# Expert phase: turning round the second layer's operands, its weights staged by ScalarE, and the first layer's weights staged by a transfer inside the chip

## The chip, the cores and the metric

One NeuronCore of a Trainium2 chip runs the whole program; the other cores stand idle. The metric is the device time of one execution in microseconds (us). Below, PE is TensorE (matrix multiplies and transposes), ACT is ScalarE, DVE is VectorE, POOL is GpSimd, SP is SyncE, which here only issues transfers and waits.

## The reference

A block of a transformer over x of 32 x 256 tokens with 128 channels (8,192 tokens): normalisation, causal attention with 16 heads, normalisation, residual; then a mixture of 8 experts, of which each token uses one; normalisation, residual. The part that matters here is the expert step.

```python
feats = x.reshape(-1, 128)
expert = argmax(feats @ centroids.T, axis=1)          # E = 8
alpha = sigmoid(sum(feats * centroids[expert], -1))
h = normalise(feats) * gamma[e] + beta[e]
y = feats + relu(h @ W1[e].T + b1[e]) @ W2[e].T + b2[e]   # W1[e]: 512 x 128, W2[e]: 128 x 512
out = alpha * y + (1 - alpha) * feats
```

## The kernel before, in words

**Attention phase.** Blocks of 256 tokens; each has 8 slots (two heads each), and every engine runs the same software pipeline over the slots. The last 16 slots (`not live(0)` in the code) only drain it, and work that prepares the expert phase is laid into them: the first layer's weights are split into two fp32r parts that add up to fp32 (`w1`, at L788 on ACT and L1005 on DVE), the biases are folded (L595 on PE), and the second bias b2 is turned into rows: eight fp32 products with the identity on PE (L711), a copy on ACT into `b2row`, and on DVE the low half and the selector `picks` (L1012, L1014). In the same slots the last two blocks are routed: each token's expert, its destination row, and a row of 260 numbers written to `routed_rows` in HBM, sorted by expert. When the count of each expert is known (`ends`, L999 on DVE), SP writes eight pads behind the experts' rows (L244), and POOL writes the last block's rows (L1210) after those have landed.

**Expert phase.** `table` gives for each of 39 tiles of 256 rows its start row and its expert. A tile goes through slots; `live(n)` in `slot` means that the tile n slots back is handled here. `ffn_phases` writes 8 slots out for the first 8 tiles, then loops over 3 x 8 slots, then writes out the rest. Order per slot s on each engine:

- SP loads the rows of tile s into `fin` (8 buffers, in the trace as `softmax`; L262), once POOL has finished with tile s-8.
- PE: two transposes of tile s into `psN` (L278), then the first layer of tile s-1: 12 fp32r matmuls, stationary `w1st`, moving the turned tokens in two parts, 256 columns each (L292), then the second layer of tile s-2: per half of 128 tokens one product with `picks` and `b2row` for the bias (L303) and four fp32 products, **stationary the hidden activations, moving the weights** straight out of `wx` at the expert's address, 128 columns (L306). The result has tokens on the partitions.
- ACT: the high part of the turned tokens (`xt_hi` in the trace), the square root for tile s-4 (`gsd`, L330), the copy of the expert's first-layer weights, 128 x 1024, into `w1st` (in the trace `p_both<-w`, two buffers), two of the four relu blocks of tile s-1 (L345), a copy of b1.
- DVE: the low part (`xt_lo`, L395), residual and statistics of tile s-3 (L405 to L415), the other two relu blocks of tile s-1 (L423), the final normalisation of tile s-4 (L429, L434).
- POOL: adds the residual for tile s-4 (L449), copies the row numbers, and scatters the tile before it to `out` with two indirect transfers (L456).

An instruction waits for semaphores by count, so the order written here is the order in which each engine runs. PE waits before L292 for the relus of tile s-2 (`relu_a`, `relu_d`), ACT before `xt_hi` for the transposes (`n_tr`).

## Time and profile before

| | us |
|---|---|
| median of 3 runs | 1291.23 (1290.55 to 1293.27) |
| the profiled execution, its own time | 1290.58 |
| its span in the trace | 1286.4 |
| PE busy | 1221.9 (95%) |
| DVE busy | 1130.4 (88%) |
| ACT busy | 1062.5 (83%) |
| POOL busy | 924.2 (72%) |

The span runs from the first to the last instruction; 4.2 us of the device time lie around it. The expert phase is what comes after 1104.7 us: the first matmul on a loaded tile starts there.

### The profile page before, as it was taken

How to read it: one execution, taken by the hardware profiler on the slowest of the kernel's cores; microseconds unless marked ns; L12 is line 12 of the kernel's file. 1: busy time of each engine (PE TensorE's matmuls, PEld its weight loads, DVE VectorE, ACT ScalarE, POOL GpSimd, SP SyncE). 2: the span in 40 equal slices, each digit the busy share in tenths (PEclk: the TensorE clock that was granted, in tenths of full speed). 3: DMA queues.
4: the chain of work that ended last, by engine and by line, in shares of the span. 5: the costliest groups of instructions: out<-in, count | busy, mean ns of one | idle time of the engine just before them, and what ended most of it. 6: DMA issues, size and time to landing. Idle time of an engine off the chain costs nothing.

```text
span 1286.4 us, 42145 instructions
## 1 busy us (share of the span) xinstructions
PE 1221.9 (95%) x12784; PEld 1105.4 (86%) x12785; DVE 1130.4 (88%) x4457; ACT 1062.5 (83%) x3244; POOL 924.2 (72%) x1495
## 2 busy tenths in 40 slices
PE   7999999999999999999999999999999997599992
PEld 6888888888888888888888888888888886599982
DVE  5999999999999999999999999999999995488873
ACT  4999898999999999999999999999999893466661
POOL 4577777777777777777777777777777665067775
PEclk8999999999999999999999999999999997799997
DMA  5000000000000000000000000000000003333320
GB/s 228 6 10 18 16 16 16 16 16 16 16 16 16 16 16 16 16 16 16 16 16 16 16 16 16 13 16 14 15 16 13 15 15 123 98 97 101 96 84 13
DMA packets 39233, 43.03 MB, mean 33 GB/s; under 512 B 4802, under 2 KB 35398, under 8 KB 38800
## 3 DMA queue, kind: packets, MB, share of 16 engines
q1 hardware_dynamic: 33536, 29.43, 7.6%
q0 software_dynamic: 5648, 13.00, 2.7%
q8 instruction: 25, 0.41, 0.1%
q14 instruction: 24, 0.20, 0.1%
HBM read 25.16 MB, written 18.16 MB: 34 GB/s over the span
## 4 chain that ended last, share of the span: by engine, by line
PE 86%; issue 5%; POOL 3%; DVE 1%; ACT 1%; SPq 1%; DMA 1%; POOLq 0%; ACTq 0%; DVEq 0%
PE psZU L682 17%; PE psS L605 14%; PE psZU L697 14%; PE psP L649 10%; PE psZU L685 7%; PE psT L619 5%; PE psT L620 5%; PE psT L621 5%; PE psS L292 3%; POOL out L456 2%; PE psZU L306 2%; PE psT L306 1%; PE psP L584 1%; PE psM L736 1%; PE psM L727 1%
## 5 line engine op out<-in xcount | busy, mean ns | idle before, releaser
L1219 POOL TENSOR_TENSOR softmax<-softmax,rinv 128x256 f32<-128x256 f32 (+1 forms) x512 | 413.2, 828 | 213.8 <-DVE rinv L947 213.0
L781 ACT ACTIVATE softmax<-softmax,nmax 128x128 f32<-128x128 f32 (+1 forms) x1024 | 453.8, 451 | 9.1 <-DVE nmax L923 8.3
L923 DVE CUSTOM_DVE_ANT_0 softmax<-psS,mask 128x128 f32<-128x128 f32 (+1 forms) x1024 | 321.6, 352 | 5.6 <-PE psS L605 1.1
L932 DVE TENSOR_TENSOR p_both<-psP,p_both 128x768 fp32r<-128x768 f32 x256 | 243.8, 952 | 0.9 <-ACT p_both L745 0.9
L745 ACT ACTIVATE t_hi<-psT 128x512 fp32r<-128x512 f32 x256 | 153.0, 598 | 84.0 <-PE psT L621 78.0
L911 DVE TENSOR_TENSOR t_lo<-psT,t_hi 128x512 fp32r<-128x512 f32 x256 | 175.3, 685 | 41.9 <-ACT t_hi L745 40.8
L745 ACT ACTIVATE p_both<-psP 128x768 fp32r<-128x768 f32 x256 | 206.6, 807 | 2.3 <-PE psP L649 2.3
L781 ACT ACTIVATION_READ_ACCUMULATOR softmax<-softmax,nmax 128x1 f32 x1024 | 199.1, 194 | 0.0
L952 DVE TENSOR_TENSOR z_lo<-psZU,z_hi 128x512 fp32r<-128x512 f32 x256 | 175.3, 685 | 20.0 <-ACT z_hi L745 18.1
L605 PE MATMUL psS<-t_hi,t_lo 64*128 64x128 f32 (+1 forms) x1024 | 164.5, 317 | 0.4 <-DVE nmax L923 0.4
L682 PE MATMUL psZU<-p_both,xk_hi 128*128 128x512 f32 x512 | 160.7, 395 | 0.0
L619 PE MATMUL psT<-xt_hi,qk_lo 128*128 128x256 f32 x512 | 150.0, 293 | 2.3 <-DVE t_lo L911 1.2
L745 ACT ACTIVATE z_hi<-psZU 128x512 fp32r<-128x512 f32 x256 | 148.6, 581 | 1.5 <-PE psZU L685 1.5
L649 PE MATMUL psP<-ident,softmax 64*128 64x64 f32 x3072 | 147.8, 229 | 0.5 <-DVE p_both L932 0.5
L697 PE MATMUL psZU<-z_hi,b_lo 128*128 128x256 f32 x512 | 145.7, 285 | 0.0
L697 PE MATMUL psZU<-z_hi,b_hi 128*128 128x256 f32 x512 | 143.3, 280 | 0.0
L620 PE MATMUL psT<-xt_lo,qk_hi 128*128 128x256 f32 x512 | 143.3, 280 | 0.0
L605 PE MATMUL psS<-t_lo,t_hi 64*128 64x128 f32 (+1 forms) x1024 | 143.2, 275 | 0.0
L621 PE MATMUL psT<-xt_hi,qk_hi 128*128 128x256 f32 x512 | 143.0, 279 | 0.0
L697 PE MATMUL psZU<-z_lo,b_hi 128*128 128x256 f32 x512 | 142.6, 278 | 0.0
L605 PE MATMUL psS<-t_hi 64*128 64x128 f32 (+1 forms) x1024 | 142.6, 274 | 0.0
L649 PEld LDWEIGHTS psP<-ident,softmax 64*128 64x128 f32 x3072 | 116.0, 139 | 26.4 <-issue 0.7
(197 smaller groups left out, 3192.0 us busy)
## 6 DMA issues: line engine op xcount, KB each, us to landing
softmax<-routed_rows SPq DMA_DIRECT2D x39, 260.0 KB, 2.7
routed_rows<-padr SPq DMA_DIRECT2D x8, 520.0 KB, 4.9
wx<-ffn_w SPq DMA_DIRECT2D x2, 2058.0 KB, 13.0
xin<-x SPq DMA_DIRECT2D x32, 128.0 KB, 2.2
xres<-x SPq DMA_DIRECT2D x32, 128.0 KB, 2.1
out<-wq_s,ids POOLq DMA_INDIRECT x78
wup_s<-wup SPq DMA_DIRECT2D x1, 1024.0 KB, 5.9
routed_rows<-pay,dst POOLq DMA_INDIRECT x64
```

Source lines behind the costliest of these rows:

```text
L605: last = mm(psS[:, e, a:z], qq[h, tb, 0, q * P:(q + 1) * P], kk[h, tb, 1, 0:z - a], start=(n == 0), stop=(n == 2))
L619: mm(psT[:, m, :], qk_lo[:, r, m, :], xt_hi[:, db, :], start=True, stop=False)
L620: mm(psT[:, m, :], qk_hi[:, r, m, :], xt_lo[:, db, :], start=False, stop=False)
L621: last = mm(psT[:, m, :], qk_hi[:, r, m, :], xt_hi[:, db, :], start=False, stop=True)
L649: last = nc.tensor.transpose(psP[:, e, 64 * n:64 * n + 64], prob[half, s % 4, h, k * P:(k + 1) * P], ident[half, half])
L682: mm(psZ[:, :, :], xx[:, zx, 0, :], pp[:, zb, :, 0:T], start=(n == 0), stop=False, skip_group_check=True)
L697: last = mm(psU[:, 0:T], bb[:, hh, :], zz[:, ub, h, :], start=(ur == 0 and h == 0 and n == 0), stop=(ur == PAIRS - 1 and h == 1 and n == 2))
L745: cp = lambda o, i: nc.scalar.activation(o, i, ACT.Copy)
L781: last = nc.scalar.activation(prob[:, pb, h, a:z], nscore[:, (s - lag) % 2, h, a:z], ACT.Exp, bias=nmax[:, pb, h, q:q + 1], scale=-1.0, ac ...
L923: last = v.tensor_tensor_reduce(nscore[:, n1, h, a:z], psS[:, h, a:z], mask[:, a:z], -1.0, -MASKED, ALU.add, ALU.min, nmax[:, p1, h, q:q + 1])
L932: v.tensor_tensor(by_half(p_lo, s % 2), psPh, by_half(p_hi, s % 2).bitcast(F32), ALU.subtract).then_inc(S["p_split"], 1)
L1219: last = g.tensor_tensor(pr, pr, rinv[:, p2, :, q:q + 1].broadcast_to([P, 2, z - a]), ALU.mult)
```

## The change

In words:

- **Second layer turned round.** ACT copies the expert's b1, W2 and b2 (517 columns) out of `wx` into `w2st` (4 buffers) once per tile. PE now runs four fp32 products per tile with the **weights stationary and the hidden activations moving**, 256 columns each; the result `psY` has channels on the partitions. ACT copies it to `yt` and adds b2 as a bias; in the next slot PE turns it back with two transposes into `psO`. Everything behind it (DVE's statistics, POOL's scatter) moves one slot later; the phase has one slot more.
- **First layer's weights by a transfer.** ACT's copy of 128 x 1024 goes; SP issues a transfer of the same 512 KB inside the chip's memory, behind the load of tile s, at an address from a register, after the first layer of tile s-2.
- **b2 as rows is gone**, with `picks`: the L711, `b2row` and L1012/L1014 work in the draining slots, and PE's register load in each slot.

```diff
-        B2 = W2 + FB * P
-        b1st = sb("b1st", [P, 4, FB])
-        b2row = sb("b2row", [P, E, P], F32R)
-        picks = sb("picks", [P, P], F32R)
+        W2W = FB + FB * P + 1
+        w2st = sb("w2st", [P, 4, W2W])
         assert 2 * HD == 2 * FB * T and HD // P == 2 * FB
         hid = wup_s[:].rearrange("p (b j t) -> p b j t", b=2, j=FB)
+        yt = sb("yt", [P, T])
         gst = sb("gst", [P, 2, 6])
         carry = sb("carry", [P, 1])
         gmv = sb("gmv", [P, 2, 2, 2])
         gsd = sb("gsd", [P, 2, 2])
         grs = sb("grs", [P, 2, 2])
-        for n in """pads_ready pad_stored ends_ready table_steps table_ready w1_hi_done w1_split w1st_ready b1st_ready
-            b2_turned b2_hi_done b2_split
-            nt_hi_done nt_ready relu_a relu_d n_tr h_done y_done g_steps gmv_ready gsd_ready
+        for n in """pads_ready pad_stored ends_ready table_steps table_ready w1_hi_done w1_split w2st_ready
+            nt_hi_done nt_ready relu_a relu_d n_tr h_done yt_done yt_ready y_tr g_steps gmv_ready gsd_ready
             grs_ready on_ready res_ready ids_ready""".split():
             S[n] = sem(n)
 
+        w1_loaded = [sem(f"w1_loaded{i}") for i in range(2)]
...
-        psN, psY = psU, (psT, psZ)
+        psN, psY, psO = psU, psT, psZ
...
-            for s in range(rest + 5 - FU):
+            for s in range(rest + 6 - FU):
...
+                if live(2):
+                    sp.wait_ge(S["h_done"], m0 + s - 1)
+                elif s == 0:
+                    sp.wait_ge(S["w1_split"], E)
+                e = sp.value_load(table[0:1, bass.ds(m0 + s, 1), 1], min_val=0, max_val=E - 1)
+                sp.dma_start(w1st[:, s % 2].rearrange("p m f -> p (m f)").bitcast(F32),
+                             w1[:, bass.ds(e, 1)].rearrange("p a m f -> p (a m f)").bitcast(F32)
+                             ).then_inc(w1_loaded[s % 2], 16)
...
-                if live(2):
-                    e = pe.value_load(table[0:1, bass.ds(m0 + s - 2, 1), 1], min_val=0, max_val=E - 1)
                 if live(1):
 
                     pe.wait_ge(S["nt_ready"], m0 + s)
-                    pe.wait_ge(S["w1st_ready"], m0 + s)
+                    pe.wait_ge(w1_loaded[(s - 1) % 2], 8 * m0 + 16 * ((s + 1) // 2))
                     if live(2):
                         pe.wait_ge(S["relu_a"], m0 + s - 1)
                         pe.wait_ge(S["relu_d"], m0 + s - 1)
@@ -292,21 +295,26 @@
                             last = mm(psH[:, j, :], w1st[:, b, m, j * P:(j + 1) * P], nt[:, b, :],
                                       start=(n == 0), stop=(n == 2))
                     last.then_inc(S["h_done"], 1)
-                if live(2):
-
-                    pe.wait_ge(S["relu_a"], m0 + s - 1)
-                    pe.wait_ge(S["relu_d"], m0 + s - 1)
+                if live(3):
+
+                    pe.wait_ge(S["yt_ready"], m0 + s - 2)
                     if live(4):
                         pe.wait_ge(S["g_steps"], 2 * (m0 + s - 3) - 1)
                     for t in range(2):
-                        y = psY[s % 2][:, t, 0:P]
-                        mm(y, picks[:], b2row[:, bass.ds(e, 1), :].rearrange("p a c -> p (a c)"), start=True, stop=False)
-                        for j in range(FB):
-                            a = W2 + j * P
-                            last = mm(y, hid[:, s % 2, j, t * P:(t + 1) * P],
-                                      wx[:, bass.ds(e, 1), a:a + P].rearrange("p a c -> p (a c)"),
-                                      start=False, stop=(j == FB - 1))
-                    last.then_inc(S["y_done"], 1)
+                        last = nc.tensor.transpose(psO[:, t, 0:P], yt[:, t * P:(t + 1) * P], ident[:])
+                    last.then_inc(S["y_tr"], 1)
+                if live(2):
+
+                    pe.wait_ge(S["relu_a"], m0 + s - 1)
+                    pe.wait_ge(S["relu_d"], m0 + s - 1)
+                    pe.wait_ge(S["w2st_ready"], m0 + s - 1)
+                    if live(3):
+                        pe.wait_ge(S["yt_ready"], m0 + s - 2)
+                    for j in range(FB):
+                        a = FB + j * P
+                        last = mm(psY[:, 0, :], w2st[:, (s - 2) % 4, a:a + P], hid[:, s % 2, j, :],
+                                  start=(j == 0), stop=(j == FB - 1))
+                    last.then_inc(S["yt_done"], 1)
...
+                if live(3):
+                    act.wait_ge(S["yt_done"], m0 + s - 2)
+                    if live(4):
+                        act.wait_ge(S["y_tr"], m0 + s - 3)
+                    nc.scalar.activation(yt[:], psY[:, 0, :], ACT.Identity,
+                                         bias=w2st[:, (s - 3) % 4, W2W - 1:W2W]).then_inc(S["yt_ready"], 1)
+                if live(5):
+                    b, sf = (s - 5) % 2, (s - 5) % FU
+                    act.wait_ge(S["gmv_ready"], m0 + s - 4)
                     for t in range(2):
                         last = nc.scalar.activation(gsd[:, b, t:t + 1], gmv[:, b, t, 1:2], ACT.Sqrt,
                                                     bias=fin[:, sf, t, C_EPS:C_EPS + 1])
                     last.then_inc(S["gsd_ready"], 1)
+                if live(1):
+                    act.wait_ge(S["h_done"], m0 + s)
+                    act.wait_ge(S["w2st_ready"], m0 + s)
+                    if live(3):
+                        act.wait_ge(S["yt_done"], m0 + s - 2)
+                    for j in range(2):
+                        last = nc.scalar.activation(hid[:, (s - 1) % 2, j, :], psH[:, j, :], ACT.Relu,
+                                                    bias=w2st[:, (s - 1) % 4, j:j + 1])
+                    last.then_inc(S["relu_a"], 1)
                 if live(0):
                     e = act.value_load(table[0:1, bass.ds(m0 + s, 1), 1], min_val=0, max_val=E - 1)
-                    if live(2):
-                        act.wait_ge(S["h_done"], m0 + s - 1)
-                    cp(w1st[:, s % 2].rearrange("p m f -> p (m f)"),
-                       w1[:, bass.ds(e, 1)].rearrange("p a m f -> p (a m f)")).then_inc(S["w1st_ready"], 1)
-                if live(1):
-                    act.wait_ge(S["h_done"], m0 + s)
-                    act.wait_ge(S["b1st_ready"], m0 + s)
-                    if live(3):
-                        act.wait_ge(S["y_done"], m0 + s - 2)
-                    for j in range(2):
-                        last = nc.scalar.activation(hid[:, (s - 1) % 2, j, :], psH[:, j, :], ACT.Relu,
-                                                    bias=b1st[:, (s - 1) % 4, j:j + 1])
-                    last.then_inc(S["relu_a"], 1)
-                if live(0):
                     if live(4):
+                        act.wait_ge(S["yt_done"], m0 + s - 3)
                         act.wait_ge(S["relu_d"], m0 + s - 3)
-                    cp(b1st[:, s % 4, :], wx[:, bass.ds(e, 1), B1:W2].rearrange("p a c -> p (a c)")
-                       ).then_inc(S["b1st_ready"], 1)
+                    cp(w2st[:, s % 4, :], wx[:, bass.ds(e, 1), B1:].rearrange("p a c -> p (a c)")
+                       ).then_inc(S["w2st_ready"], 1)
...
-                if live(3):
-
-                    b, sf = (s - 3) % 2, (s - 3) % FU
-                    m = m0 + s - 3
-                    dve.wait_ge(S["y_done"], m + 1)
-                    if live(5):
+                if live(4):
+
+                    b, sf = s % 2, (s - 4) % FU
+                    m = m0 + s - 4
+                    dve.wait_ge(S["y_tr"], m + 1)
+                    if live(6):
                         dve.wait_ge(S["on_ready"], m - 1)
                     for t in range(2):
-                        last = v.scalar_tensor_tensor(gg[:, b, t, :], psY[b][:, t, 0:P], fin[:, sf, t, C_GAIN:C_GAIN + 1],
+                        last = v.scalar_tensor_tensor(gg[:, b, t, :], psO[:, t, 0:P], fin[:, sf, t, C_GAIN:C_GAIN + 1],
...
-                if live(4):
-                    b = s % 2
-                    dve.wait_ge(S["gsd_ready"], m0 + s - 3)
+                if live(5):
+                    b = (s - 5) % 2
+                    dve.wait_ge(S["gsd_ready"], m0 + s - 4)
...
-                if live(4):
-                    m, b, c, sf = m0 + s - 4, s % 2, s % 4, (s - 4) % FU
+                if live(5):
+                    m, b, c, sf = m0 + s - 5, (s - 5) % 2, (s - 5) % 4, (s - 5) % FU
...
-                if not live(0) and s == 4:
-                    pe.wait_ge(S["nmax_ready"], 2 * PAIRS * NB)
-                    for e in range(E):
-                        last = mm(psS[:, e // 4, (e % 4) * P:(e % 4 + 1) * P],
-                                  wx[:, e, B2:B2 + 1].broadcast_to([P, P]), ident[:], start=True, stop=True)
-                    last.then_inc(S["b2_turned"], 1)
...
-                if not live(0) and s == 5:
-                    act.wait_ge(S["b2_turned"], 1)
-                    for n in range(2):
-                        last = cp(b2row[:, 4 * n:4 * n + 4, :].rearrange("p e c -> p (e c)"), psS[:, n, :])
-                    last.then_inc(S["b2_hi_done"], 1)
...
-                if not live(0) and s == 6:
-
-                    dve.wait_ge(S["b2_hi_done"], 1)
-                    low = slice(P // 2, P)
-                    v.tensor_tensor(picks[:], ident[:, 0:1].broadcast_to([P, P]),
-                                    ident[:, P // 2:P // 2 + 1].broadcast_to([P, P]), ALU.add)
-                    v.tensor_tensor(b2row[low].rearrange("p e c -> p (e c)"), psS[low].rearrange("p n k -> p (n k)"),
-                                    b2row[low].rearrange("p e c -> p (e c)").bitcast(F32),
-                                    ALU.subtract).then_inc(S["b2_split"], 1)
```

How the rows stand on the engines. First PE in the draining slots of the attention phase, where b2 was turned (`psM<-cent` scores the routed tokens, `psT<-bet,wx` folds a bias). Before:

```order
L697 MATMUL psZU<-z_hi,b_hi 128x256
L595 MATMUL psT<-bet,wx 128x1 x4
L711 MATMUL psS<-ident,wx 128x128 [waits nmax_ready]
L711 MATMUL psS<-ident,wx 128x128 x7
L727 MATMUL psM<-cent,ft 128x8 [waits a_norm,ft_ready]
L727 MATMUL psM<-cent,ft 128x8
L697 MATMUL psZU<-z_hi,b_lo 128x256 [waits z_split]
L697 MATMUL psZU<-z_lo,b_hi 128x256
```

Of the change:

```order
L707 MATMUL psZU<-z_hi,b_hi 128x256
L605 MATMUL psT<-bet,wx 128x1 x4
L731 MATMUL psM<-cent,ft 128x8 [waits a_norm,ft_ready]
L731 MATMUL psM<-cent,ft 128x8
L707 MATMUL psZU<-z_hi,b_lo 128x256 [waits z_split]
L707 MATMUL psZU<-z_lo,b_hi 128x256
```

The two rows with `ident,wx` are gone; the scoring product stands right behind the bias folding.

Second, PE in one slot of the loop over tiles. Before, the end of the first layer and the first half of the second (`wup_s` holds the hidden activations):

```order
L292 MATMUL psS<-xt_hi,p_both 128x256
L300 ISA [waits relu_d,relu_a]
L303 ISA [waits g_steps]
L303 MATMUL psT<-b2row,picks 128x128
L306 ISA
L306 MATMUL psT<-wx,wup_s 128x128
L306 ISA
L306 MATMUL psT<-wx,wup_s 128x128
L306 ISA
L306 MATMUL psT<-wx,wup_s 128x128
L306 ISA
L306 MATMUL psT<-wx,wup_s 128x128
```

Of the change, the end of the first layer and all of the second, then the next slot's transposes:

```order
L295 MATMUL psS<-xt_hi,p_both 128x256
L300 REGISTER_ALU
L302 ISA [waits yt_ready]
L304 MATMUL psZU<-ident,yt 128x128 [waits g_steps]
L304 MATMUL psZU<-ident,yt 128x128
L315 MATMUL psT<-wup_s,w2st 128x256 [waits w2st_ready,yt_ready,relu_d,relu_a]
L315 MATMUL psT<-wup_s,w2st 128x256 x3
L281 REGISTER_ALU [waits f_loaded1]
L283 MATMUL psZU<-ident,softmax 128x128 [waits nt_ready]
L283 MATMUL psZU<-ident,softmax 128x128
```

The two products with `picks` and the eight of 128 columns per slot (the piece shows the first half of them) have become four of 256 columns, with the two transposes of the tile before ahead of them, which wait for `yt_ready`.

Third, SP in one slot of the loop. Before:

```order
L256 ISA [waits ids_ready,res_ready]
L256 TENSOR_LOAD table
L256 ISA x2
L262 ISA
L262 DMA softmax<-routed_rows 128x2x260
```

Of the change:

```order
L255 ISA [waits ids_ready,res_ready]
L255 TENSOR_LOAD table
L255 ISA x2
L261 ISA
L261 DMA softmax<-routed_rows 128x2x260
L267 ISA [waits h_done]
L267 TENSOR_LOAD table
L267 ISA x2
L268 ISA
L268 DMA p_both<-w 128x1024
```

Between two loads of tiles SP now waits for `h_done`, reads the expert's number and issues the transfer of the weights; all of them stand in one queue.

## Rows read from the trace of the kernel before

**Rows 1.** Loop: length, busy PE, PEld, DVE, ACT, POOL, clock, DMA share, GB/s.

```profile
1141.80:1235.90 94.10, 89.58 (x770) 87.29 (x769) 76.25 (x310) 62.56 (x168) 68.60 (x97) 1.00 0.34 99
```

**Rows 2.** Who waited for whom, 1110 to 1250 us: total, times, longest.

```profile
ACT xt_hi L320 <- PE psZU L278: 41.8, 32, 2.1
...
PEld psS L292 <- issue: 11.9, 17, 1.8
```

**Rows 3.** Timeline of two slots in the loop: start, duration, engine, line.

```profile
1169.88 0.60 DVE L434 TENSOR_SCALAR xres<-xin,gmv,grs 128x128 f32<-128x128 f32 x2
...
1170.68 0.74 POOL L449 TENSOR_TENSOR wq_s<-xres,softmax 128x256 f32<-128x256 f32 x1 [1.31 <-DVE xres L434]
...
1173.00 0.98 POOL L456 DMA_INDIRECT out<-wq_s,ids  x1 [0.31 <-issue]
...
1173.32 0.38 PE L278 MATMUL psZU<-ident,softmax 128*128 128x128 f32 x2
...
1174.67 0.39 ACT L320 ACTIVATE xt_hi<-psZU 128x256 fp32r<-128x256 f32 x1 [1.94 <-PE psZU L278]
...
1175.09 0.42 DVE L395 TENSOR_TENSOR xt_lo<-psZU,xt_hi 128x256 fp32r<-128x256 f32 x1 [1.06 <-ACT xt_hi L320]
...
1176.81 0.84 DVE L423 TENSOR_SCALAR wup_s<-psS,b1st 128x256 f32<-128x256 f32 x2
...
1176.92 0.38 PE L278 MATMUL psZU<-ident,softmax 128*128 128x128 f32 x2
...
1177.76 0.60 DVE L434 TENSOR_SCALAR xres<-xin,gmv,grs 128x128 f32<-128x128 f32 x2
...
1177.80 0.36 PE L292 MATMUL psS<-xt_hi,p_both 128*128 128x256 f32 x1 [0.50 <-issue]
```

**Rows 4.** Timeline of an early slot, before POOL's first scatter.

```profile
1118.78 0.38 PE L278 MATMUL psZU<-ident,softmax 128*128 128x128 f32 x2
...
1119.20 0.38 ACT L320 ACTIVATE xt_hi<-psZU 128x256 fp32r<-128x256 f32 x1 [1.07 <-PE psZU L278]
```

**Rows 5.** Groups by shape, 1141.8 to 1235.9 us: count, busy us, mean ns.

```profile
L320 ACT ACTIVATE p_both<-w 128x1024 fp32r x24 | 25.4, 1058 | 0.3
```

**Rows 6.** Timeline of PE's weight loads for fp32 products of 512 columns.

```profile
8.27 0.19 PEld L546 LDWEIGHTS psS<-wup_s,wd_s 128*128 128x128 f32 x1 [0.24 <-issue]
8.70 0.32 PEld L546 LDWEIGHTS psS<-wup_s,wd_s 128*128 128x128 f32 x1 [0.24 <-issue]
```

**Rows 7.** Chain that ended last, from the draining slots: start, us, what.

```profile
1072.87 1.89 PE psS L711 x16
...
1077.37 0.20 DVE picks L1012
1077.58 1.23 DVE b2row L1014
...
1080.01 0.46 SPq L243
...
1092.60 4.77 DMA routed_rows<-padr
```

**Rows 8.** Page, transfers by line: count, KB each, median us from issue to landing.

```profile
softmax<-routed_rows SPq DMA_DIRECT2D x39, 260.0 KB, 2.7
```

**Rows 9.** Transfers of the first 30 us, same columns.

```profile
wo_s<-wo SPq DMA_DIRECT2D x1, 512.0 KB, 7.5
```

**Rows 10.** Timeline of the first tiles.

```profile
1101.83 8.32 SPq L262 DMA_DIRECT2D softmax<-routed_rows  x8
...
1107.66 0.55 PE L292 MATMUL psS<-xt_hi,p_both 128*128 128x256 f32 x1 [0.44 <-ACT p_both L320]
```

**Rows 11.** Timeline of POOL at the end.

```profile
1262.38 0.72 POOL L449 TENSOR_TENSOR wq_s<-xres,softmax 128x256 f32<-128x256 f32 x1 [1.63 <-DVE xres L434]
...
1269.06 0.74 POOL L449 TENSOR_TENSOR wq_s<-xres,softmax 128x256 f32<-128x256 f32 x1
...
1272.37 0.74 POOL L449 TENSOR_TENSOR wq_s<-xres,softmax 128x256 f32<-128x256 f32 x1
```

More of the change, by code:

```diff
@@ L268, in ffn_pe @@
             mm = nc.tensor.matmul
-            pe.wait_ge(S["table_ready"], 1)
-            pe.wait_ge(S["b2_split"], 1)
             def slot(m0, n0, s, live):
@@ L294, in slot @@
                     last.then_inc(S["h_done"], 1)
+                if live(3):
+                    pe.wait_ge(S["yt_ready"], m0 + s - 2)
+                    if live(4):
+                        pe.wait_ge(S["g_steps"], 2 * (m0 + s - 3) - 1)
+                    for t in range(2):
+                        last = nc.tensor.transpose(psO[:, t, 0:P], yt[:, t * P:(t + 1) * P], ident[:])
+                    last.then_inc(S["y_tr"], 1)
                 if live(2):
@@ L450, in slot @@
                     g.tensor_copy(ids[:, c, :], fin[:, sf, :, C_ID].bitcast(U32)).then_inc(S["ids_ready"], 1)
-                if live(5):
-                    m5, c5 = m0 + s - 5, (s - 5) % 4
-                    wait_apart(pool, S["res_ready"], m5 + 1)
-                    pool.wait_ge(S["ids_ready"], m5 + 1)
+                if live(6):
+                    m6, c6 = m0 + s - 6, (s - 6) % 4
+                    wait_apart(pool, S["res_ready"], m6 + 1)
+                    pool.wait_ge(S["ids_ready"], m6 + 1)
                     for t in range(2):
-                        g.indirect_dma_start(out, bass.IndirectOffsetOnAxis(ap=ids[:, c5, t:t + 1], axis=0),
-                                             res[:, c5, t, :], None, bounds_check=ntok - 1,
-                                             oob_is_err=False).then_inc(stored[(s - 5) % FU], 16)
+                        g.indirect_dma_start(out, bass.IndirectOffsetOnAxis(ap=ids[:, c6, t:t + 1], axis=0),
+                                             res[:, c6, t, :], None, bounds_check=ntok - 1,
+                                             oob_is_err=False).then_inc(stored[(s - 6) % FU], 16)
             ffn_phases(pool, slot)
```

19 lines of the change are left out of this document (7 added, 12 removed).

## The prediction

> **What bounds the kernel now.** I read the busy time by stage first. In the loop over tiles 24 tiles take 94.1 us, 3.92 us each; TensorE is busy for 95% of it at full clock, which looks like the bound [rows 1, 5]. The waits say otherwise: ScalarE waits 41.8 us in 32 slots for the transposes of L278, and the weight loads of the first layer stand still 17 times, 11.9 us in all [rows 2]. The timeline shows why. From one L278 to the next without a stall TensorE needs 3.60 us (1173.32 to 1176.92), 0.32 less than the period. It then stands until 1177.80, because VectorE's relus end at 1176.81 + 0.84 = 1177.65 [rows 3]. These are late because `xt_lo` began at 1175.09, behind `xt_hi` at 1174.67; and `xt_hi` began 1.35 us after L278, although in an early slot it begins 0.42 us after it [rows 3, 4].
>
> What holds it for the other 0.93 us? In the early slot GpSimd does not scatter yet. In the loop the late start always comes some 0.7 us after the end of the pair of indirect transfers (1173.00 + 0.98 = 1173.98, then 1174.67) [rows 3]. I take it that TensorE's signal for the transposes comes through only when GpSimd's pair is away. That closes a ring: VectorE's last operation on a tile ends at 1170.48; GpSimd's residual starts at 1170.68, its pair ends at 1173.98, `xt_hi` starts at 1174.67 (4.19 us); `xt_lo` at 1175.09 (0.42); VectorE's slot runs to 1177.76 + 0.60 = 1178.36 (3.27). The ring is 7.88 us and spans two slots: 3.94 per tile, against 3.92 measured [rows 1, 3, 5]. So the bound of the loop is this ring, and TensorE has 0.3 us per tile to spare.
>
> The draining slots matter too. The chain runs from TensorE's L711 through VectorE's `b2row` to the expert counts, SyncE's pads and their landing; POOL's last rows and the first tile wait for that [rows 7].
>
> **The change part by part.**
>
> *b2 rows gone.* On the chain L711 takes 1.89 us, `picks` 0.20 and `b2row` 1.23: 3.32 [rows 7]. I take 0.1 off, since VectorE's own work ahead of the scores now ends about when they come. Pads and first load move with it: -3.2. Bounds: -1.4 if the scores do not come forward, -3.3.
>
> *Second layer on TensorE.* The slot of 3.60 us holds 32 loads with their products (2 transposes, 12, 2 with `picks`, 16 halves of fp32 products), 0.1125 each. An fp32 product is two loads; with 512 columns a half takes 8.70 - 8.27 = 0.43 [rows 6], so 0.215 with 256. New slot: 16 x 0.1125 + 8 x 0.215 = 3.52, so 0.08 less. Since the ring sets the pace, it buys nothing: 0 (if TensorE did, -0.08 x 36 = -3, 36 being the 39 tiles less the first three).
>
> *The turned result.* `yt` is copied behind `xt_hi`, so TensorE can turn it only some 0.9 us after the late signal, and stands about 0.7 us in the slots in which its first layer ended early. The work behind that (second layer 1.72, transposes 0.22) ends 3.35 us after the signal, before the next one is due at 3.94. Cost 0; without that cover up to 0.7 in every second slot, 13 us.
>
> *ScalarE.* Away: the copy of 1.06 us [rows 5] and that of b1. New: 517 columns, between 0.54 (half of 1.06) and 1.06, and `yt`, about 0.4 like `xt_hi` [rows 3]. It is busy 62.56/24 = 2.6 us of 3.92 [rows 1] and stays near that: 0.
>
> *The weights' transfer.* Issued when the first layer of tile s-2 ends, needed at the first layer of tile s: two periods less one first layer, 2 x 3.92 - 1.4 = 6.4 us. SyncE issues one load each 1.04 us (8 in 8.32) [rows 10]; so issue 1.0, then landing between 2.7 (260 KB) and 7.5 (512 KB behind other loads) [rows 8, 9]. I take 3.5, nearer the first since the queue is short: 4.5 in all, hidden. The load of tile s+1 stands behind it in the queue: issued at 2.1, landed at about 5.6 with the transfer's 1.4 ahead, wanted at 6.3. Hidden too, by 0.7. As a check only: the Trainium skill ("DMA: Bandwidth & Descriptors", Anatomy of one DMA) puts a transfer at 2.0 us plus bytes over 436 GB/s. By that rule 512 KB would be an estimated 3.2 us; no row here shows a transfer from the core's memory to itself, and the sum is the same.
>
> *First tiles.* The first layer starts 5.83 us after the first load is issued, behind ScalarE's copy [rows 10]. Now tile 1's load stands behind 512 KB: about +0.1 there; tile 3's load waits for the first layer of tile 0 and its weights: about +0.4 more. Sum +0.5 (-1 to +2).
>
> *End.* Everything behind the second layer is a slot deeper, so GpSimd has one tile more when TensorE is done. Back to back it needs 3.31 us per tile (1269.06 to 1272.37), but it waited 1.63 before 1262.38 [rows 11], which the extra tile fills: +1.7 (0 to +3.3).
>
> Sum: -3.2 + 0.5 + 1.7 = -1.0. Span 1286.4 - 1.0 = 1285.4, own time of that execution 1290.58 - 1.0 = 1289.6; it lies 0.65 under the median of the runs, so 1290.2.
>
> **The rivals.**
>
> *A. TensorE sets the pace after all, or the new phases slip out of the ring.* For it: 95% busy, and a signal that is late for GpSimd's sake is inferred from its timing alone. Against: the ring's sum meets the period within 0.02, and the stall before L292 would not exist. If the signal came through at once, TensorE's 3.52 us would bound (VectorE's 3.27 is less): 3.55 a tile, 0.37 x 36 = -13.3, with the rest -14: 1277. The Trainium skill ("TensorE: Matmul & The Clock Gate", The cost: per-tile semaphore tail) gives a tail of 25 ns plus 26 ns per increment, and strict order of completion. By that rule a signal would never be 0.9 us late, and the time would be rival A's; rows 3 against rows 4 speak against it. Chance 0.27.
>
> *B. Transfers late (slower).* SyncE's one queue now carries 772 KB per tile, and each pair starts only at `h_done`. The ring is: signal, issue, both landings, transposes 0.2, first layer 1.4, two slots long. It decides once the landing of tile s+1's load comes more than 6.3 us after `h_done`. With 7.5 for the transfer as in rows 9, plus issue, it is 8.5 + 1.6 = 10.1 per two slots, 5.05 each: +40 us. Nearer the rows of short queues, 7.0 us gives 4.3: +0.38 x 36 = +14, less 1: 1304. Or the denser traffic holds TensorE's other signals in the same way (`h_done` too, then the relus start late), which costs the same order. For it: margin of 0.7 only, 39 x 512 KB more beside a DMA share of 0.34 [rows 1]. Chance 0.28.
>
> *C. The middle stays, the ends differ.* Ramp and end at their bounds: 1287 to 1294. That is the forecast's own range. Chance 0.45 with the forecast.
>
> **How the numbers follow.** A measurement of this kernel tells some 0.2%, 2.6 us, from no change. The forecast's case (0.45) gives faster 0.09, same 0.33, slower 0.03; A gives 0.25 faster and 0.02 same; B gives 0.27 slower and 0.01 same. So faster 0.34, same 0.36, slower 0.30. The likeliest case has 1287 to 1294 as its own range; eight in ten need most of A and B: 1277 to 1303.
>
> **What would show it.** In the changed trace: the count landed in `ends` about 3.2 us earlier, near 1076.8, and the first L278 of a tile near 1101.6; in the loop still 3.9 us per tile, `xt_hi` starting about 0.7 us after the end of GpSimd's pair, and the first layer standing for VectorE's relus; waits for DMA on TensorE near nil after the first four tiles; the fp32 halves 0.215 us apart; GpSimd back to back for six tiles at the end. The prediction is wrong if the period of the loop moves: below 3.8 my reading of the ring is wrong; above 4.0 with TensorE waiting for `softmax` or `p_both` it is rival B.

## The result, and the profile after

The changed kernel takes 1292.66 us (median of 20 runs, 1290.39 to 1295.44), the kernel before, beside it on the same chip, 1290.29 us (20 runs, 1288.17 to 1293.38): 1.0018 times, interval 1.001 to 1.0027. So it is 2.4 us slower; I had forecast 1290.2, 1 us faster. The profiled execution of the change took 1290.56 us, 2.1 below its own median, with a span of 1286.3 us beside 1286.4 before.

The equal spans hide large parts of both signs. Stages, each read from the starts of the transposes of the tiles (L278 before, L283 after) or from the rows named:

| stage | before | after | difference | forecast |
|---|---|---|---|---|
| start to the last bias products ahead of the scores | 1071.92 | 1068.54 | -3.4 | 0 |
| from there to the count in `ends` | 7.90 | 3.99 | -3.9 | -3.2 |
| `ends` to the first tile's transposes | 24.97 | 24.20 | -0.8 | 0 |
| tiles 0 to 8 | 29.24 | 31.93 | +2.7 | +0.5 |
| tiles 8 to 32 (the loop) | 93.81 | 96.67 | +2.9 | 0 |
| tiles 32 to 38 | 25.43 | 26.14 | +0.7 | 0 |
| last tile's transposes to the end | 33.13 | 34.83 | +1.7 | +1.7 |

The first line is no part of the change. In the execution profiled before, TensorE's granted clock was 0.59 between 8 and 12 us and 0.57 between 22 and 26 us; after, it was 1.00 in both stretches. The first puts the kernel before 2.1 us behind, the second another 1.1; from 27 us on the lag is 3.15 us and stays between 3.1 and 3.4 through the whole attention phase. Without it the sum is +3.3, near the +2.4 of the medians.

The loop, as [rows 1], for the same 24 tiles (10 to 34), and its waits, as [rows 2] (total, times, longest):

```profile
1136.78:1235.57 98.79, 93.94 (x577) 79.97 (x577) 76.56 (x313) 60.83 (x168) 68.67 (x97) 1.00 0.65 221
```

```profile
ACT xt_hi L328 <- PE psZU L283: 28.9, 24, 1.7
...
PEld psZU L304 <- issue: 5.4, 21, 0.5
...
PEld psZU L283 <- issue: 5.1, 8, 0.8
PE psZU L283 <- DMA softmax<-routed_rows: 2.4, 6, 0.9
```

4.12 us a tile beside 3.92; the DMA share has gone from 0.34 to 0.65. The stall ahead of the first layer (L292) of [rows 2] is gone. Two others stand there: in nearly every slot 0.26 us ahead of L304, the transposes of the turned result, and in some slots 0.6 us and more ahead of L283, for the row load. One slot of the changed kernel (timeline, as [rows 3]):

```profile
1169.33 0.38 PE L283 MATMUL psZU<-ident,softmax 128*128 128x128 f32 x2
...
1169.75 0.39 ACT L328 ACTIVATE xt_hi<-psZU 128x256 fp32r<-128x256 f32 x1 [1.04 <-PE psZU L283]
...
1170.16 0.42 DVE L405 TENSOR_TENSOR xt_lo<-psZU,xt_hi 128x256 fp32r<-128x256 f32 x1 [0.62 <-ACT xt_hi L328]
...
1170.50 0.60 DVE L415 SCALAR_TENSOR_TENSOR xin<-psZU,softmax 128x128 f32<-128x128 f32 x2
...
1170.77 0.39 SPq L261 DMA_DIRECT2D softmax<-routed_rows  x1
...
1171.16 0.44 PE L304 MATMUL psZU<-ident,yt 128*128 128x128 f32 x2
...
1171.43 1.91 PE L315 MATMUL psT<-wup_s,w2st 128*128 128x256 f32 x8
...
1171.98 0.71 SPq L268 DMA_DIRECT2D p_both<-w  x1
...
1173.60 0.43 PE L283 MATMUL psZU<-ident,softmax 128*128 128x128 f32 x2 [0.26 <-DMA softmax<-routed_rows]
```

`xt_hi` now starts 0.42 us after L283; the late signal of [rows 3] does not appear. But L304 starts at 1171.16, just behind the end of L415 (1170.50 + 0.60 = 1171.10). The code says why: `psO` is one buffer, so L304 waits (`g_steps`) until VectorE has read the turned result of the tile before, and on VectorE that read stands behind `xt_lo`, which stands behind this slot's own L283. That is a ring of one slot: L283 to `xt_hi` 0.42, to `xt_lo` 0.41, to L415 0.34, its 0.60, to L304 0.06, to L315 0.27, L315 to the next L283 1.79 (1167.54 to 1169.33, the slot before): 3.89. Of the 24 slots from tile 8 to 32, 15 are 3.84 to 3.95, with a mean of 3.88.

The row load that the last line waits for was issued at 1170.77, 2.8 us before. SyncE had waited for `h_done`, read the expert's number and issued the weights' transfer at 1168.69 first. Seven of the 24 slots are late in this way, 4.25 to 4.43 us. In six of them the row load left SyncE only 3.50 to 4.07 us after the end of the first layer that it follows (median of all 24: 2.75) and was wanted 2.8 to 3.0 us later; in the seventh (tile 13) it left after 2.6 and took 3.7 to be there.

Which of the two costs what, on this chip? 24 slots of 3.88 would be 93.1 us, 0.7 less than the 93.81 before. The seven late ones have 3.2 us more than that, two others (4.03 and 4.09) 0.4. So against the kernel before the +2.9 of the loop is the late row loads; the new ring only stands where the old one stood, at nearly the same length.

The first tiles, from the windows view of the change and of the kernel before (columns of [rows 1]):

```profile
1104.73:1106.73 2.00, 2.00 (x10) 2.00 (x10) 0.08 (x1) 0.08 (x1) 0.00 (x0) 0.50 1.00 322
1106.73:1108.73 2.00, 2.00 (x7) 1.59 (x7) 0.80 (x2) 1.28 (x3) 0.00 (x0) 0.64 0.22 78
```

```profile
1108.79:1110.79 2.00, 2.00 (x11) 1.79 (x9) 0.19 (x1) 0.36 (x2) 0.00 (x0) 0.50 0.87 237
1110.79:1112.79 2.00, 1.30 (x10) 1.14 (x10) 1.11 (x3) 1.96 (x5) 0.00 (x0) 0.90 0.63 192
```

TensorE enters the phase at the lower level, 1.2 GHz. Before, the clock rose at 1111.2, 6.4 us behind the first transposes (1104.79); in the change it rose at 1108.2, 11.5 us behind them (1096.73), and tile 3 starts 6.83 us behind tile 2 where it was 4.82. The clock is not the only cause. The row load of tile 3 was also late:

```profile
1104.54 0.38 SPq L261 DMA_DIRECT2D softmax<-routed_rows  x1
...
1109.21 0.20 PEld L283 LDWEIGHTS psZU<-ident,softmax 128*128 128x128 f32 x2 [0.44 <-DMA softmax<-routed_rows]
```

By its semaphore it landed at 1109.17, 4.63 us after its issue, where those of tiles 0 to 2 took 2.7 to 2.8; the weights' transfer just ahead of it (1103.29) took 5.3, where the two before it took 3.0 and 3.1. TensorE's work at the low clock ended at the same moment, so either alone would have given this gap (the experiments show it below).

The tail of the attention phase, from VectorE's timeline before, then after:

```profile
1076.62 0.75 DVE L1005 SCALAR_TENSOR_TENSOR w<-wx,gam,w 128x512 fp32r<-128x512 f32 x1 [0.48 <-ACT w L788]
1077.28 0.28 DVE L1012 TENSOR_TENSOR picks<-ident 128x128 fp32r<-128x128 f32 x1
1077.58 1.23 DVE L1014 TENSOR_TENSOR b2row<-psS,b2row 64x1024 fp32r<-64x1024 f32 x1
...
1079.82 0.16 DVE L999 CAST ends<-base 128x8 int32<-128x8 f32 x1
```

```profile
1071.03 0.75 DVE L1004 SCALAR_TENSOR_TENSOR w<-wx,gam,w 128x512 fp32r<-128x512 f32 x1
...
1072.53 0.16 DVE L998 CAST ends<-base 128x8 int32<-128x8 f32 x1
```

Besides the 3.3 us of L711, `picks` and `b2row`, the 0.48 us is gone for which VectorE waited for ScalarE's `w`, because ScalarE had `b2row` to copy first. At the end GpSimd runs back to back, as forecast, 3.32 us a tile (compare [rows 11]):

```profile
1258.97 0.74 POOL L459 TENSOR_TENSOR wq_s<-xres,softmax 128x256 f32<-128x256 f32 x1
...
1262.29 0.74 POOL L459 TENSOR_TENSOR wq_s<-xres,softmax 128x256 f32<-128x256 f32 x1
...
1272.23 0.74 POOL L459 TENSOR_TENSOR wq_s<-xres,softmax 128x256 f32<-128x256 f32 x1
```

### The profile page after: what moved, and what is told of

Same layout as the page of the kernel before. It is cut to its first block, busy times and chain, and to the rows that moved or that the text cites. A ratio compares the mean times of both kernels' runs of the same rounds, so it can differ in the third digit from the quotient of the medians.

```text
span 1286.3 us, 41459 instructions
## 1 busy us (share of the span) xinstructions
PE 1223.8 (95%) x12456; PEld 1090.2 (85%) x12456; DVE 1128.7 (88%) x4455; ACT 1058.0 (82%) x3242; POOL 923.7 (72%) x1495
## 4 chain that ended last, share of the span: by engine, by line
PE 82%; issue 6%; SPq 3%; POOL 2%; DMA 2%; DVE 2%; ACT 1%; POOLq 0%; DVEq 0%; ACTq 0%
PE psZU L692 17%; PE psS L615 14%; PE psZU L707 14%; PE psP L659 10%; PE psZU L695 7%; PE psT L629 5%; PE psT L630 5%; PE psT L631 5%; POOL out L466 2%; PE psP L594 1%; PE psS L295 1%; PE psT L315 1%; PE psM L740 1%; PE psM L731 1%; DMA out<-wq_s,ids 1%
```

## The experiments

Each group of runs has runs of the kernel before beside it on the same chip, and the ratio is to those. The chips were of two kinds. On kind A (the prediction's) the kernel before takes 1289 to 1290 us, on kind B 1281 to 1282. So ratios are compared within a kind only. The three last columns are from the profiled execution: the 24 slots from tile 8 to 32, the shortest of them, and last transposes to the end.

| run | kind, before | median | ratio, interval | tiles 8 to 32 | shortest | end |
|---|---|---|---|---|---|---|
| the change | A 1290.3 | 1292.7 | 1.0018, 1.0010-1.0027 | 96.67 | 3.84 | 34.8 |
| e12 one scatter again | A 1288.9 | 1276.4 | 0.9892, 0.9873-0.9912 | 87.36 | 3.64 | 29.3 |
| e13 load first | A 1289.7 | 1294.3 | 1.0041, 1.0026-1.0055 | 96.58 | 3.59 | 33.9 |
| e14 change, one scatter | A 1289.7 | 1284.4 | 0.9954, 0.9938-0.9970 | 94.44 | 3.84 | 30.1 |
| e5 before again | B 1281.4 | 1281.2 | 1.0002, 0.9989-1.0015 | 87.35 | 3.63 | 33.1 |
| e6 change again | B 1281.4 | 1290.5 | 1.0071, 1.0054-1.0089 | 94.56 | 3.84 | 34.8 |
| e7 second layer alone | B 1281.4 | 1286.0 | 1.0034, 1.0021-1.0047 | 92.94 | 3.84 | 34.8 |
| e8 transfer alone | B 1281.4 | 1299.5 | 1.0146, 1.0128-1.0165 | 101.06 | 3.59 | 33.3 |
| e1 rows ahead | B 1280.7 | 1288.0 | 1.0051, 1.0038-1.0063 | 93.00 | 3.84 | 34.8 |
| e2 two buffers | B 1280.7 | 1284.1 | 1.0026, 1.0016-1.0035 | 90.19 | 3.53 | 34.9 |
| e3 both | B 1280.7 | 1281.4 | 1.0002, 0.9993-1.0011 | 88.13 | 3.54 | 34.7 |
| e4 ScalarE issues | B 1280.7 | 1288.4 | 1.0055, 1.0043-1.0067 | 93.32 | 3.84 | 36.4 |
| e9 b2 later | B 1282.1 | 1277.3 | 0.9964, 0.9951-0.9976 | 87.36 | 3.64 | 33.1 |
| e10 second alone, two buffers | B 1282.1 | 1276.5 | 0.9957, 0.9941-0.9974 | 85.62 | 3.54 | 34.8 |
| e11 one scatter | B 1282.1 | 1275.6 | 0.9951, 0.9935-0.9968 | 87.35 | 3.63 | 29.5 |

**The order of SyncE's queue, and the ring (e1 to e4, kind B).** Rows ahead (`rows_of` reads the start row of a tile and issues its load, as SyncE's slot did):

```diff
+            rows_of(0, 0)
...
-                row = sp.value_load(table[0:1, bass.ds(m0 + s, 1), 0], min_val=0, max_val=E * REGION)
...
+                if live(-1):
...
+                    rows_of(m0 + s + 1, (s + 1) % FU)
                 if live(2):
                     sp.wait_ge(S["h_done"], m0 + s - 1)
```

> The changed kernel, but SyncE issues the row load of tile s+1 ahead of the weights' transfer of tile s instead of behind it. Theory 1 (SyncE's order): in the changed kernel a row load leaves only some 2.8 us before it is wanted, because SyncE needs about 3.5 us from the end of a first layer to the next row load; 8 of 25 slots of the loop are 4.3 us instead of 3.85, and tiles 3 and 34 come 2 us late. Then all these waits go: 8 x 0.45 + 2 + 2 = 7.6 us less than the changed kernel, about 1285. Rival (contention): the transfers themselves are slow since 772 KB per tile share the engines; then the row loads stay late by as much and the time stays within 2 us of the changed kernel's 1292.7.

Two buffers for the turned result:

```diff
-        psN, psY, psO = psU, psT, psZ
+        psN, psY = psU, psT
+        psO = (psZ, psP[:, 0, :].rearrange("p (h q) -> p h q", h=2))
...
-                    if live(4):
-                        pe.wait_ge(S["g_steps"], 2 * (m0 + s - 3) - 1)
+                    if live(5):
+                        pe.wait_ge(S["g_steps"], 2 * (m0 + s - 4) - 1)
...
```

The transposes write the two by turns and VectorE reads them by turns.

> The changed kernel, but the turned result has two PSUM buffers by turns, so TensorE's transposes of it need not wait for VectorE's read of the tile before. Theory 1 (a new ring): the slots of 3.85 us without a DMA wait are set by transposes, high part, low part, VectorE's first operation on the turned result, transposes of the turned result, second layer; with two buffers TensorE needs 3.55. Since the row loads then are late more often, only part shows: 0 to 4 us less than 1292.7. Rival (TensorE's own work takes 3.85): no difference, and the slots without a DMA wait stay 3.85.

> Both edits: row loads issued ahead of the weights' transfer, and two PSUM buffers for the turned result. Theory 1: slots of the loop go to 3.55 (TensorE's own work), 0.3 x 35 = 10 us less than with the row loads ahead alone, about 1275. Rival A (TensorE's own work takes 3.85): the same as with the row loads ahead alone, about 1285. Rival B (TensorE's signals held until GpSimd's pair of scatters is away, as I read the kernel before): slots of two lengths again, 3.7 to 3.9 on average, the high part late by about 1 us in every second slot, 1281 to 1287.

ScalarE issues the transfer (`weights_of` reads the expert's number and issues it):

```diff
                     last.then_inc(S["relu_a"], 1)
+                if live(-1):
+                    weights_of(m0 + s + 1, (s + 1) % 2)
```

> The changed kernel, but ScalarE issues the weights' transfer, behind the relus of the tile whose weights it overwrites; SyncE keeps only the row loads. Theory 1 (SyncE's order): the row loads' lateness goes as with row loads ahead, about 1285, if the issue costs ScalarE less than 1 us per tile (it is busy 2.5 of 3.9). Rival (contention of the transfers): no change, 1292. Rival (ScalarE's issue and register load lie on the ring): relus and the staging copy late, slots of 4.0 and more, slower than 1292.

The shapes came as theory 1 has them. With the rows ahead no slot of the loop is over 4.1 us (two in e6, seven in the change on kind A), with two buffers slots of 3.53 to 3.59 appear, and both together give 88.13 us for the 24. With ScalarE as issuer the late slots are gone too, but it gains nothing over e1. My sizes were off: the gaps at tiles 3 and 34 stay in e1 (6.66 and 5.57 us), so it gains 0.2% on the change (2.5 us, on two chips of kind B) and not 7.6 us. e2 gained 6.4 us on e6 (expected 0 to 4), e3 6.6 on e1 (expected 10). In e1 the row load of tile 3 was there early (issued at 1101.54), so its gap comes with the low clock; so does e7's, without any transfer (6.93). At tile 34 the loop ends, and VectorE stands 2.4 us before its L430 with no releaser in the trace; what holds it there I did not test.

**Why these ratios are above 1.0018, and the parts alone (e5 to e8, kind B).**

> The kernel before, unchanged, for its trace on the chip of these runs: there it took 1280.65 us, on the first chip 1290.3. Theory 1: the expert phase differs; TensorE's slots are 3.6 to 3.7 us in the loop (no late signal in every second slot), so the ring that I read on the first chip is not a fixed property of the kernel. Then the phase from the first to the last transposes is about 138 to 142 us instead of 148.5, the high part starts 0.4 us after the transposes. Rival: the attention phase or the end is shorter and the loop is 3.92 per tile as on the first chip.

The loop of the kernel before runs at 3.64 us flat on this chip, TensorE without a pause (windows, then the timeline that answers to [rows 3]):

```profile
1132.58:1219.93 87.35, 87.35 (x770) 87.35 (x769) 76.94 (x313) 62.79 (x168) 67.92 (x97) 1.00 0.37 106
```

```profile
1172.03 0.97 POOL L456 DMA_INDIRECT out<-wq_s,ids  x1 [0.30 <-issue]
...
1172.62 0.38 PE L278 MATMUL psZU<-ident,softmax 128*128 128x128 f32 x2
...
1173.03 0.38 ACT L320 ACTIVATE xt_hi<-psZU 128x256 fp32r<-128x256 f32 x1 [1.02 <-PE psZU L278]
```

GpSimd's second transfer is under way at L278 here as well, yet `xt_hi` starts 0.41 us behind L278, not 1.35. On kind A it is late in the short slots too: in 23 of the loop's 24 slots it starts 0.99 to 1.52 us behind L278; only the length of the slots alternates. So the ring of the kernel before belongs to chips of kind A.

> The changed kernel, unchanged, on the same chip as the others. If the new ring (3.85 per slot) and SyncE's late row loads set its pace, it has no part in what makes the kernel before faster there: 1291 to 1293, so about 0.9% slower than the kernel before there. Rival: it gains as the kernel before does, and stands 0.2% above it.

It does not gain: 94.56 us for the 24 slots, 2 less than on kind A. Span against span it is 8.5 us over e5: first transposes 5.2 earlier, tiles 0 to 8 +2.7, 8 to 32 +7.2, 32 to 38 +2.2, end +1.7. Second layer alone (ScalarE copies `w1st` between `gsd` and the relus, SyncE's transfer is gone) and transfer alone (the kernel before, with SyncE's lines and TensorE's wait of the change in place of ScalarE's copy):

> The second layer's part of the change alone: weights stationary, turned result, but ScalarE still copies the first layer's weights (128x1024) and no transfer is issued. Theory 1: ScalarE is busy 0.39 + 0.47 + 0.48 + 1.06 + 0.84 + 0.64 = 3.9 us per tile with its copy ahead of the relus, so the relus come 1.1 us later and the period is 4.0 or more: slower than the changed kernel by up to 5 us. Rival (only the row loads behind the transfer matter): slots flat at 3.85, 6 to 8 us less than the changed kernel.

> The first layer's part alone: the kernel before, with its second layer and b2 rows as they were, but SyncE issues the transfer of the first layer's weights as in the change. Theory 1 (SyncE's order): the row loads come late as in the changed kernel, with gaps at tiles 3 and 34, so 4 to 8 us slower than the kernel before. Rival (the row loads were late only because TensorE's slots have changed): no difference to the kernel before, since its slots alternate and the wait is covered.

e7 has slots of 3.84 to 4.03 in the loop with ScalarE 85% busy: the copy of 1.06 us did fit, against theory 1. Without the transfer the kernel is 4.5 us below e6 by the medians; the traces show 2.1 of these in the phase. e8 is the surprise: 18 us, twice the whole change. Its timeline:

```profile
1168.22 0.39 PE L287 MATMUL psZU<-ident,softmax 128*128 128x128 f32 x2
...
1169.88 0.36 PE L301 MATMUL psS<-xt_hi,p_both 128*128 128x256 f32 x1 [1.27 <-DVE xt_lo L400]
```

Its L301 works on the tile before, whose inputs had long been there. TensorE's own instructions between the two (start, ns; not in the groups above, since register work does not count as busy):

```
1168.083   36 Tensor ALU_OP        L285 (wait for the row load)
1168.337  908 Tensor TENSOR_LOAD   L290 (expert's number for the second layer)
1169.303  151 Tensor FUSED_REGOPS  L290
1169.682   36 Tensor ALU_OP        L296 (wait for the weights)
1169.854  186 Tensor LDWEIGHTS     L301
```

The register load stands behind the wait for the row load. In the kernel before it takes 291 ns at 1171.68, 1.6 us ahead of the transposes it follows in the program (1173.32), so nothing waits for it. In e8, of the 23 loads that the trace holds between 1130 and 1230 us, the four that start behind the transposes take 0.91 to 0.95 us, and six that start up to 0.15 us ahead of them 0.44 to 0.55.

**What each part is worth (e9 to e11, kind B).** b2 later (in the kernel before, L711, ScalarE's `b2row` copies, `picks` and L1014 moved to the start of each engine's expert phase), second layer alone with two buffers, and one scatter (half of the output rows are not written; GpSimd's waits for landed scatters count half as many):

```diff
-                    for t in range(2):
+                    for t in range(1):
                         g.indirect_dma_start(out, bass.IndirectOffsetOnAxis(ap=ids[:, c5, t:t + 1], axis=0),
...
```

> The kernel before, with the turning of b2 into rows (L711, b2row, picks) moved behind the attention phase on each engine, where TensorE, ScalarE and VectorE stand while SyncE writes its pads; second layer and first layer's weights as before. Theory 1: the change's only gain is the chain to the expert counts, 3.9 us shorter, and it can be had without the rest; 3.9 us (0.3%) less than the kernel before, with pads earlier by as much. Rival: the three pieces then end later than the first tiles want them, and half or more of the gain is lost.

> The second layer's part alone as in the earlier run (ScalarE copies the first layer's weights, no transfer), with two PSUM buffers for the turned result. Theory 1: without the ring TensorE's 3.55 to 3.6 sets the slots, as ScalarE's 3.3 us per tile still fits: the phase from the first to the last transposes goes from 150.1 to 141 us or less, 9 us less than with one buffer. Rival: ScalarE, then 92% busy with the relus behind its copy, becomes the bound, slots of 3.75 and more, and the gain is under 5 us.

> The kernel before with one of the two scatters of each tile left out, so half of the output rows are not written. Where the kernel before runs at 3.64 us per slot (TensorE's work), nothing changes in the loop, and the end gets shorter by 1 to 3 us. Where it runs at 3.6 and 4.2 to 4.4 by turns (as on the first chip), my reading of that kernel (a signal held until GpSimd's pair is away) gives 3.64 flat, 7 us less for the loop; the rival reading (the signal is late for a cause that has nothing to do with the scatters) leaves the alternation as it is.

e9 takes the gain of the tail and nothing else: loop and end as e5, span 4.8 us less. e10 has the shortest loop of all, 3.57 us a slot (windows, then timeline):

```profile
1130.05:1215.67 85.62, 85.62 (x577) 79.55 (x576) 77.31 (x313) 79.55 (x193) 67.46 (x97) 1.00 0.37 107
```

```profile
1172.89 0.38 PE L276 MATMUL psZU<-ident,softmax 128*128 128x128 f32 x2
...
1174.07 0.60 DVE L413 SCALAR_TENSOR_TENSOR xin<-psZU,softmax 128x128 f32<-128x128 f32 x2
...
1174.48 0.38 PE L297 MATMUL psP<-ident,yt 128*128 128x128 f32 x2
```

L297 starts at 1174.48, while VectorE's read of the other buffer (L413) still runs until 1174.67: the ring is open. ScalarE is 93% busy and still no bound. Both e9 and e10 are faster than the two kernels of this case on kind B; neither was run on kind A. e11 tells nothing of the loop on kind B, as expected; its end is 3.6 us shorter (expected 1 to 3), and the time outside the span is 1.8 us where it was 4.2.

**One scatter on kind A (e12).**

> The same kernel with one scatter per tile (half of the output rows are not written), once more, in case it runs where the kernel before takes 1290 us. There, my reading (the signal is held until GpSimd's pair is away) gives slots of 3.64 us flat, and a time near the 1275.6 of the earlier run; the rival (late for another cause) keeps slots of 3.6 and 4.2 by turns, near 1283. Where the kernel before takes 1281 us again, the run repeats the earlier one, 1275 to 1276, and tells the readings not apart.

All slots of the loop are 3.64 us, and the time is 12.5 us less than the kernel before, where on kind B the same edit gave 6.5. With half the scatters gone kind A runs like kind B (1276.4 and 1275.6). `xt_hi` starts 0.42 to 0.50 us behind L278 in all 24. So the late signal and the alternation of [rows 3] come from GpSimd's pair of scatters.

**The load first, and the change with one scatter (e13 and e14, kind A).** TensorE's register load ahead of the wait for the row load, on e8, and the change with one scatter:

```diff
             def slot(m0, n0, s, live):
+                if live(2):
+                    e = pe.value_load(table[0:1, bass.ds(m0 + s - 2, 1), 1], min_val=0, max_val=E - 1)
                 if live(0):
                     pe.wait_ge(f_loaded[s], n0 + 16)
...
-                if live(2):
-                    e = pe.value_load(table[0:1, bass.ds(m0 + s - 2, 1), 1], min_val=0, max_val=E - 1)
```

> The transfer alone (kernel before with the weights' transfer), but TensorE's register load of the expert stands ahead of the wait for the row load instead of behind it. Theory 1: each late row load costs the lateness and then 1.3 to 1.7 us more, since the register load (0.9 us), its address work and the first layer can only follow it; with the load first the slots of 4.4 to 5.2 go to 4.0 and less, 10 us or more less than the transfer alone, 1285 to 1290 where the kernel before takes 1281. Rival (the lateness of the transfers alone costs the 18 us): no more than 3 us less.

> The changed kernel with one of the two scatters per tile left out (half of the output rows are not written). The end gets shorter by about 3.5 us in any case, since GpSimd has less to do there. Theory 1 (SyncE's own instructions make the row loads late; the ring of the turned result sets 3.85): the loop stays at 3.85 to 3.95 per slot, 3 to 5 us less than the changed kernel in all. Rival (GpSimd's scatters hold SyncE up): where the kernel before takes 1290, the slots of 4.3 go, 3 to 4 us more; where it takes 1281 there are few such slots and nothing to tell.

e13 is 0.41% above the kernel before, e8 was 1.46% above it on the other kind; the 24 slots take 96.58 us instead of 101.06, although kind A is the slower one for this layout. All of TensorE's register loads from 1130 to 1230 us take 0.29 to 0.31 us in it. That agrees with theory 1, but compares across kinds.

e14 keeps the ring (shortest slot 3.84) and ends 4.7 us sooner; three of the 24 slots are over 4.1 us instead of seven. Each against the kernel before beside it, e14 is 7.7 us below the change, where theory 1 alone had 3 to 5. In the profiled executions 2.5 lie outside the span and 2.2 in the 24 slots. A count in the traces goes with the slots: of SyncE's register and wait instructions from 1130 to 1230 us, those over 500 ns are 23 in the change on kind A, 2 in e6, 2 in e14. Register loads are no proof by themselves (e1, on kind B, has 23 that long, e3 20), but without them the count is 10 in the change, and 0 in e6, e1, e3 and e14. So the rival was right in part: GpSimd's scatters held SyncE up too.

**The first tiles, from all traces.** e14 also separates the two causes at tile 3. Its clock was back 5.8 us behind the first transposes, and yet its gap is 6.82 us, because the row load issued at 1106.70 landed at 1111.33:

```profile
1111.37 0.64 PE L283 MATMUL psZU<-ident,softmax 128*128 128x128 f32 x2 [2.11 <-DMA softmax<-routed_rows]
```

| at tile 3 | clock back early (5 to 7 us) | clock back late (11 to 12 us) |
|---|---|---|
| row load there in time | 4.55 (e3, e4), 4.82 (e5) | 6.65 (e1), 6.93 (e7) |
| row load 4.6 us under way | 6.82 (e14) | 6.83 (the change), 6.82 (e6), 6.94 (e2) |

The clock came back late in 6 of the 9 executions with the turned second layer and in 2 of the 7 with the old one (e11 and e12, gaps of 7.12 and 6.98), so it is not the change's alone. Why these two transfers take 5.3 and 4.6 us in the change, e2, e6 and e14 stays open.

## Why the prediction was wrong, step by step

- **The weights' transfer, "hidden, by 0.7"**: on the chip of the forecast this step failed. The landing was right: it takes 3.0 us (1097.93 to 1100.94), where I had 3.5; the Trainium skill ("DMA: Bandwidth & Descriptors", Anatomy of one DMA) gave an estimated 3.2 by a rule that it fits to transfers issued by GpSimd, and this one, issued by SyncE, agrees. But the next row load leaves SyncE 3.5 us after the first layer's end (1167.25 to 1170.77), or 2.75 in the slot after, where I had 2.1. That used up the margin: seven slots of 4.25 to 4.43 us, 3.2 us in all, which is the +2.9 of the loop. By the prediction's own sign (above 4.0 per tile, 4.12 measured, with TensorE waiting for `softmax`) it is rival B, in small. On kind B, where the load leaves after 2.2 us in most slots, only two slots are late, and e1 and e4 remove them.
- **The turned result, "cost 0"**: the mechanism was wrong. I looked for the wait for `yt`, and found it covered by the old ring. The wait that binds is the second one of the same instruction, `g_steps`: one PSUM buffer, read by VectorE behind `xt_lo` of the same slot. It holds TensorE at 3.84 to 3.95 us where its work takes 3.57. e2, e3 and e10 open that ring, and short slots appear in all three. From e7 to e10, 7.3 us of the 24 slots go. On the forecast's chip the price against the kernel before was still nothing (3.88 beside 3.91), but by luck: a new ring had the length of the old one. It took away the room that TensorE would have had there.
- **TensorE's slot, 3.52 us**: right within 0.05 (3.57 in e10, whose slots are free of stalls).
- **The bound before**: the ring of 3.94 was read rightly for that chip, as far as e12 can show it: without the pair of scatters the late signal goes and the loop falls to TensorE's 3.64. That TensorE has 0.3 us to spare holds there alone: on kind B the kernel before is TensorE's own 3.64, so the new ring costs 5.6 us in the 24 slots there (e7 against e5), the transfer 1.6 more (e6), and the change 9 us instead of 2.4.
- **b2 rows, -3.2**: -3.9 on both kinds, beyond my bound of -3.3; the missing 0.6 is mostly VectorE's wait of 0.48 us for ScalarE. Another 0.8 came between the count and the first tile, most of it from the pads' landing (4.22 us for 4.77).
- **The rivals**: the phases did slip out of the old ring, as rival A has it, but into the new one, so its 13 us did not come. Rival B, transfers late, came at a fraction of its price.
- **First tiles, +0.5**: +2.7, beyond my bound of +2. I had priced tile 3's row load at +0.4 for its place in the queue; it was under way for 4.6 us instead of 2.7. And I had not priced the clock, which stays at its lower level some 5 us longer. Each of the two makes the whole gap.
- **End, +1.7**: right, +1.7 on both kinds.

So a loss of 2.4 us on the chip of the forecast is 4.7 us won ahead of the tiles, against 2.7 + 3.6 + 1.7 = 8.0 us behind (sum +3.3; the medians say +2.4). No kernel with rows ahead or with two buffers was run on kind A, so what they would give on that chip is not shown.

## What to carry to other kernels

When an intermediate result gets an extra hop between engines, list every wait of the new instruction, the one for its output buffer first, and follow each around the other engines' program order; here a ring of one slot that closes over a single PSUM buffer costs 0.3 us per tile, and the turned layer saves TensorE 0.07 (3.64 to 3.57). A transfer that lands in time can still be dear, because the issuing queue makes the next one late, and a register load behind a wait can add its length to the lateness (0.9 us in e8). Take the part of a change that pays by itself: moving the b2 rows to where the engines stand anyway gave 0.36% without touching the loop.

## What the runs showed of the hardware that I had not expected

- The same program takes 1289 to 1290 us on some chips and 1281 to 1282 on others, and 8.4 of the 9.9 us between the spans of the two profiled executions (before, e5) lie between tile 8 and tile 38: where GpSimd's indirect transfers are under way, other engines' signals and instructions are late on kind A. `xt_hi` starts 0.99 to 1.52 us after its transposes in 23 of 24 slots, 0.41 to 0.50 on kind B. SyncE's short register and wait instructions take over 500 ns in 12 of 193 cases between 1130 and 1230 us in the kernel before on kind A, in 0 of 211 on kind B; none of the 12 is a register load. Leaving out one scatter per tile removes the late slots (e12). What in the chip does this stays open.
- A register load of TensorE took 0.29 us when it ran ahead of need; behind a wait in e8, with the denser transfers, it took up to 0.95 us.
- Two landings in the first tiles of the change took 5.3 and 4.6 us, where transfers of the same size before them took 3.0 and 2.7; e2, e6 and e14 have the same. The cause is open.
- TensorE's clock at the start drifts between executions of one program: 0.59 or 1.00 between 8 and 12 us (2.1 us of the span) and 0.57 or 1.00 between 22 and 26 us (1.1 us). Spans of two single executions can't be compared below that without looking there.
